# Seven-product weight groups in a fused graph network: down products in eight PSUM banks, the first group computed in full, reordered vector and scalar work

## The chip, the cores and the metric

The kernel runs on one core of a Trainium2 chip. The core has a TensorE (PE) for matrix products, a VectorE (DVE), a ScalarE (ACT), a GpSimd (POOL), and SyncE (SP), whose queue issues the loads. Each has its own instruction stream and runs it in order; they meet only at semaphores. Products land in PSUM, which has eight banks of 128 partitions x 512 floats; everything else lives in SBUF. The metric is the device time of one execution in microseconds.

## The reference, cut to what matters

```python
for i in range(L):                                   # L = 4 layers
    a = _attn(_ln(h, ln2_w[i], ln2_b[i]), cond, Wq[i], Wk[i], Wv[i], Wo[i])
    h = h + a
    u = _ln(h, ln3_w[i], ln3_b[i]) @ geglu_w[i] + geglu_b[i]     # (1024,512) @ (512,4096)
    val, gate = jnp.split(u, 2, axis=-1)
    f = val * jax.nn.gelu(gate, approximate=False)
    h = h + f @ ffo_w[i] + ffo_b[i]                              # (1024,2048) @ (2048,512)
```

Before the loop stands a graph convolution over 16384 edges, and another behind it. Nothing there is touched. All is float32. Each product of two matrices is made of three matrix products in a shorter format: every operand is split in a high part (`_hi`) and the rest (`_lo`), and high x high, low x high and high x low are summed in PSUM.

## The kernel before, in words

The change is in the second half of each layer, the gated MLP, and in the first instructions of a layer.

**Tiling of the MLP.** The 2048 features are cut in eight blocks of 256, q = 0 to 7, and each block in two halves of 128, c = 0 and 1. A block needs the up product (value and gate, K = 512, 1024 rows of x as two halves of 512 columns of the moving side), the gated product f, its split, and then the down product: eight row tiles of h, t = 0 to 7, each 2 x 3 = 6 matmuls of 128x512 into one bank, which VectorE adds to h (`add_down`, L1764). The down product of block q - 1 comes behind the up products of block q.

**Sets of seven products.** Block 0 is computed in full (`mlp_step`, four steps s = 0 to 3). Blocks 1 to 7 use seven block products in place of eight, in the manner of Strassen and Winograd: one *set* is the pair (q, c), its value and gate features seen as a 2 x 2 matrix of weight blocks A11, A12, A21, A22 against a 2 x 2 matrix of x blocks. A set needs sums of the weights (S1 to S4, `weight_sums` on VectorE, L1721 to L1726) and sums of the x blocks (`t_sums`, once a layer). `set_product` on TensorE makes 7 x 6 = 42 matmuls in four banks x, y, z, v; `p1_copy` (ACT) and `set_first`, `set_last` (DVE) add the partial products and form f. Sets alternate between banks 0 to 3 and 4 to 7 (`set_banks`).

**Weights.** A set's weights arrive by four loads in `stage`, one of two slots. ACT rounds three blocks to `wg_hi` (`blocks_high`, L1014) and the four sums (`sums_high`, L1020); POOL makes both low parts (`set_low`, L643 and L646) and raises `w_ok`. SP starts the load of piece r once `w_ok` counts the pieces up to r - 2. The order in a layer is: 2 down 0, 3 and 4 the sets (1, 0) and (1, 1), 5 a piece of the next layer's attention weights (`ahead`), 6 down 1, 7 and 8 the sets of block 2, and so on.

**Order around the change.** Each engine's order is written out by hand. VectorE in block q: `set_first(q, 0)`, `set_last(q, 0)`, `set_first(q, 1)`, `weight_sums(q + 1, 0)`, `set_last(q, 1)`, the additions of tiles 0 and 1 of down product q - 1, `weight_sums(q + 1, 1)`, the additions of tiles 2 to 7. `weight_sums(q + 1, 1)` overwrites `sums_s`, so it waits until POOL has read the sums of (q + 1, 0). The eight tiles of one down product go to four banks, so that tile t of 4 to 7 waits for the addition of tile t - 4:

```python
def down_bank(q, t):
    return 4 + t % 4 if q % 2 == 0 or q == MG - 1 else t % 4
```

**Start of the MLP.** The first steps of block 0 run beside the last attention group. The rest of steps 2 and 3 (24 matmuls with 256 columns and 24 with 512) waits for `x3_low(7)` (L1644), the low part of the last row tile of x, in which VectorE comes behind `t_sums` (L1700) and `t_low` (L1705).

**Opening of a layer.** TensorE makes two V products, a transpose, a K product and then the Q product, which waits for `x2_low` on VectorE (L1635), behind `x2_high` on ACT (L869). ACT rounds the raw input of the next group (`cond_high`, L692) ahead of both.

Of the kernel before, what the change touches and what calls it, by code (L numbers as in the profile page):

```python
# [5 lines left out]
def gnn_preln_kernel(  # L6
# [82 lines left out]
    with ExitStack() as ctx:  # L89
# [594 lines left out]
        def _(act):  # L684
# [170 lines left out]
            with act.Fori(0, L) as l:  # L855
# [1517 lines left out]
```

## Time and profile before

| | us |
|---|---|
| three runs | 2591.89, 2596.22, 2599.51 |
| median | 2596.22 |
| the profiled execution | 2592.8 |
| its span, first to last instruction | 2590.9 |
| PE busy in it | 2446.0 (94%) |
| DVE, ACT, POOL busy | 1786.3, 1136.1, 703.2 |
| mean granted TensorE clock | 0.973 of full |

The profiled execution is between the fastest and the median run. A matmul's row shows how long it was in the pipeline, while the next one starts sooner: what one costs is the distance between two starts.

### The profile page before, as it was taken

How to read it: one execution, taken by the hardware profiler on the slowest of the kernel's cores; microseconds unless marked ns; L12 is line 12 of the kernel's file. 1: busy time of each engine (PE TensorE's matmuls, PEld its weight loads, DVE VectorE, ACT ScalarE, POOL GpSimd, SP SyncE). 2: the span in 40 equal slices, each digit the busy share in tenths (PEclk: the TensorE clock that was granted, in tenths of full speed). 3: DMA queues.
4: the chain of work that ended last, by engine and by line, in shares of the span. 5: the costliest groups of instructions: out<-in, count | busy, mean ns of one | idle time of the engine just before them, and what ended most of it. 6: DMA issues, size and time to landing. Idle time of an engine off the chain costs nothing.

```text
span 2590.9 us, 37159 instructions
## 1 busy us (share of the span) xinstructions
PE 2446.0 (94%) x12191; PEld 2005.9 (77%) x12191; DVE 1786.3 (69%) x3238; ACT 1136.1 (44%) x2284; POOL 703.2 (27%) x521
## 2 busy tenths in 40 slices
PE   6889999989999999989999999989999999989999
PEld 5348888877777888867778888877778888877777
DVE  8996667766665677766665677766666667766666
ACT  8964434633333434633334434643334434633333
POOL 2000000165540000155541000165540000165541
PEclk8989999999999999999999999999999999999999
DMA  2021000022110000021111100022111000022112
GB/s 74 17 82 37 33 32 33 25 66 66 54 57 34 33 33 33 25 65 59 56 61 35 33 33 33 25 65 66 53 58 34 33 32 33 25 65 66 57 54 114
DMA packets 82646, 122.44 MB, mean 47 GB/s; under 512 B 5808, under 2 KB 63536, under 8 KB 77872
## 3 DMA queue, kind: packets, MB, share of 16 engines
q1 hardware_dynamic: 82480, 120.32, 14.0%
q8 instruction: 93, 1.52, 0.2%
q14 instruction: 73, 0.60, 0.1%
HBM read 116.10 MB, written 4.19 MB: 46 GB/s over the span
## 4 chain that ended last, share of the span: by engine, by line
PE 71%; DVE 11%; issue 10%; POOL 4%; ACT 3%; DMA 1%; DVEq 0%; POOLq 0%; ACTq 0%; SPq 0%
PE ps L1828 15%; PE ps L1829 14%; PE ps L1830 14%; PE ps L2147 6%; PE ps L2151 6%; PE ps L2149 6%; PE ps L2069 2%; DVE h L1764 2%; PE ps L2086 2%; PE ps L2088 2%; DVE oh_d L1347 1%; PE ps L2083 1%; DVE sums_s L1721 1%; POOL f_lo L627 1%; PE ps L1950 1%
## 5 line engine op out<-in xcount | busy, mean ns | idle before, releaser
L545 POOL TENSOR_SCALAR veps<-mv 128x1 f32<-128x1 f32 x65 | 17.4, 268 | 1011.3 <-DVE mv L1141 1011.3
L1828 PE MATMUL ps<-wf_hi,f_hi 128*128 128x512 f32 x512 | 216.0, 422 | 48.4 <-DVE h L1764 47.1
L627 POOL TENSOR_TENSOR f_lo<-ff,f_hi 128x512 fp32r<-128x512 f32 x128 | 173.6, 1358 | 245.5 <-ACT f_hi L1039 245.5
L1829 PE MATMUL ps<-wf_lo,f_hi 128*128 128x512 f32 x512 | 210.8, 412 | 0.0
L1764 DVE TENSOR_TENSOR h<-h,ps 128x512 f32<-128x512 f32 x256 | 165.3, 683 | 65.0 <-PE ps L1830 64.9
L1830 PE MATMUL ps<-wf_hi,f_lo 128*128 128x512 f32 x512 | 210.1, 410 | 0.0
L1828 PE MATMUL ps<-cond_hi,w_hi 128*128 128x512 f32 x512 | 203.6, 398 | 0.0
L2147 PE MATMUL ps<-xT_hi,wg_hi 128*128 128x512 f32 x448 | 178.5, 398 | 25.8 <-ACT full L1045 13.3
L1828 PE MATMUL ps<-w_hi,cond_hi 128*128 128x512 f32 x512 | 201.1, 393 | 0.3 <-issue 0.2
L1829 PE MATMUL ps<-cond_lo,w_hi 128*128 128x512 f32 x512 | 200.0, 391 | 0.0
L1830 PE MATMUL ps<-w_hi,cond_lo 128*128 128x512 f32 x512 | 200.0, 391 | 0.0
L1830 PE MATMUL ps<-cond_hi,w_lo 128*128 128x512 f32 x512 | 200.0, 391 | 0.0
L1829 PE MATMUL ps<-w_lo,cond_hi 128*128 128x512 f32 x512 | 199.8, 390 | 0.0
L861 ACT ACTIVATE v_hi<-ps 128x512 fp32r<-128x512 f32 x128 | 76.3, 596 | 248.3 <-PE ps L1830 248.3
L1504 DVE TENSOR_TENSOR v_lo<-ps,v_hi 128x512 fp32r<-128x512 f32 x128 | 88.6, 692 | 130.9 <-ACT v_hi L861 130.1
L2149 PE MATMUL ps<-xT_lo,wg_hi 128*128 128x512 f32 x448 | 177.2, 396 | 0.0
L2151 PE MATMUL ps<-xT_hi,wg_lo 128*128 128x512 f32 x448 | 177.2, 396 | 0.0
L646 POOL TENSOR_TENSOR wg_lo<-sums_s,wg_hi 128x1024 fp32r<-128x1024 f32 x56 | 134.0, 2393 | 142.6 <-ACT wg_hi L1020 142.6
L1828 PEld LDWEIGHTS ps<-wf_hi,f_hi 128*128 128x128 f32 x512 | 102.2, 200 | 88.0 <-DVE h L1764 67.0
L1039 ACT ACTIVATE f_hi<-ff 128x512 fp32r<-128x512 f32 x128 | 80.9, 632 | 200.3 <-DVE ff L1752 148.9
L921 ACT ACTIVATE p_exp<-ps,nmx 128x256 f32<-128x256 f32 x256 | 118.5, 469 | 102.0 <-DVE nmx L1550 101.4
L1051 ACT ACTIVATE gel<-gel,cols_sb 128x512 f32<-128x512 f32 x112 | 81.1, 724 | 144.0 <-DVE gel L1740 140.6
(304 smaller groups left out, 6795.9 us busy)
## 6 DMA issues: line engine op xcount, KB each, us to landing
stage<-in_pieces SPq DMA_DIRECT2D x82, 512.0 KB, 3.3
stage<-in_condT SPq DMA_DIRECT2D x33, 1024.0 KB, 4.8
stage<-in_pieces SPq DMA_DIRECT2D x224, 128.0 KB, 2.6
x<-in_x SPq DMA_DIRECT2D x2, 1024.0 KB, 6.6
at_s<-at SPq DMA_DIRECT2D x1, 2048.0 KB, 6.2
at16b<-at_s SPq DMA_DIRECT2D x1, 2048.0 KB, 9.9
out<-h SPq DMA_DIRECT2D x8, 256.0 KB, 2.0
bias_row<-in_rows SPq DMA_DIRECT2D x6, 256.0 KB, 3.4
```

What stands on the lines that cost most here:

```text
L627: pool.tensor_tensor(f_lo[q % 2][:, c, half * HALF:(half + 1) * HALF], ff[:, s % 2, :], bits(f_hi[q % 2][:, c, half * HALF:(half + 1) * HA ...
L646: pool.tensor_tensor(lo[:, 3:7, :], sums_s[:, :, :], bits(hi[:, 3:7, :]), ALU.subtract).then_inc(w_ok, 1)
L921: e = act.activation(pe_[:, b, :], ps[:, S_BANK, b * M:(b + 1) * M], ACT.Exp, bias=nmx[:, b:b + 1], accum_out=rsum[:, b:b + 1])
L1051: act.activation(gel[:, e, :], gel[:, e, :], ACT.Gelu, bias=gate_bias(q, c)).then_inc(gel_ok, 1)
L1504: dve.tensor_tensor(v_lo[:, slot, mc, :], ps[:, bank, :], bits(v_hi[:, slot, mc, :]), ALU.subtract).then_inc(v_ok, 1)
L1764: dve.tensor_tensor(h[:, t, :], h[:, t, :], ps[:, down_bank(q, t), :], ALU.add)\
L1828: pe.matmul(bank, l_hi, r_hi, start=(first and i == 0), stop=False)
L1829: pe.matmul(bank, l_hi, r_lo, start=False, stop=False)
L1830: end = pe.matmul(bank, l_lo, r_hi, start=False, stop=(last and i == n - 1))
L2147: pe.matmul(ps[:, bank, :], hi[:, a, r], moving[0][:, n, :], start=(first and n == 0), stop=False, skip_group_check=True)
L2149: pe.matmul(ps[:, bank, :], hi[:, a, r], moving[1][:, n, :], start=False, stop=False, skip_group_check=True)
L2151: last = pe.matmul(ps[:, bank, :], lo[:, a, r], moving[0][:, n, :], start=False, stop=(n == 1), skip_group_check=True)
```

## The change

Six edits:

1. **Down products in eight banks.** Tiles 0 to 3 go to the banks of the set (q + 1, 0) that was just read, tiles 4 to 7 to those of (q + 1, 1). No tile waits for an addition of its own product any more; tile 4 waits until f of the second set is done. The next set's four first products wait for the additions of tiles 4 to 7, one each. Down product 7 uses the same eight banks behind down product 6.
2. **Weight sums behind additions.** Additions of tiles 0, 1 and 2 come ahead of `weight_sums(q + 1, 1)`, and POOL's `set_low` starts only when the set's four sums are done.
3. **Value in PSUM.** `set_last` writes the value's sum back to its bank, not to `o_full` in SBUF.
4. **Set (1, 0) in full:** eight products, 48 matmuls (`full_product`), without weight sums, partial copies or additions. It needs one more weight block (A21), but no sums of x.
5. **Start of the MLP reordered** on ACT, DVE and POOL; POOL's `down_low(0)` waits for `x3_low(7)`.
6. **Opening reordered:** ACT takes `v_high`, `x2_high`, `v_high`, `k_high` ahead of the two `cond_high`; VectorE has `k_low` ahead of both `cond_low`. At a layer's end TensorE waits for the addition of tile 3 of down product 7.

```diff
 def down_bank(q, t):
-    return 4 + t % 4 if q % 2 == 0 or q == MG - 1 else t % 4
+    c = t // 4 if q < MG - 1 else 1 - t // 4
+    return set_banks(min(q + 1, MG - 1), c)[t % 4]
...
 def set_low(q, c):                                             # POOL
+    full_set = (q, c) == (1, 0)
+    if not full_set:
+        pool.wait_ge(s_ok, 4 * (short_set(l, q, c) + 1))
     pool.wait_ge(a_hi_ok, SETS * l + 2 * (q - 1) + c + 1)
     pool.tensor_tensor(lo[:, 0:3, :], ...)
     pool.wait_ge(w_hi_ok, FIRST_PIECES + PIECES * l + r + 1)
-    pool.tensor_tensor(lo[:, 3:7, :], sums_s[:, :, :], ...).then_inc(w_ok, 1)
+    if full_set:
+        pool.tensor_tensor(lo[:, A21, :], stage[:, r % 2, 0:256], ...).then_inc(w_ok, 1)
+    else:
+        pool.tensor_tensor(lo[:, 3:7, :], sums_s[:, :, :], ...).then_inc(w_ok, 1)
...
-pool.wait_ge(z3_ok, NT * l + NT)
+wait_apart(pool, x3_ok, 2 + NT * l + NT)
 down_low(0)
+set_low(1, 0)
 f_low(0, 0, 0, 0)
 f_low(0, 1, 0, 1)
-set_low(1, 0)
 f_low(0, 2, 1, 0)
 f_low(0, 3, 1, 1)
 set_low(1, 1)
...
+v_high(...); x2_high(...); v_high(...); k_high(...)           # ACT, opening
 raw_here(1)
 for part in range(2):
     cond_high(1, 1, part, stage)
-v_high(...); x2_high(...); v_high(...); k_high(...)
...
 down_high(0)                                                   # ACT, start of the MLP
 t_high(1, 0)
+blocks_high(1, 0)
+a21_high()
 t_high(3, 0)
 x3_high(7)
 f_high(0, 0, 0, 0)
+gelu(1)
 t_high(2, 0)
-gelu(1)
-blocks_high(1, 0)
 f_high(0, 1, 0, 1)
 for n in (1, 3, 2):
     t_high(n, 1)
-sums_high(1, 0)
 gelu(2)
 f_high(0, 2, 1, 0)
 gelu(3)
+blocks_high(1, 1)
+sums_high(1, 1)
+f_high(0, 3, 1, 1)
 t4_high()
-f_high(0, 3, 1, 1)
-blocks_high(1, 1)
-p1_copy(1, 0)
-sums_high(1, 1)
...
-dve.scalar_tensor_tensor(value, ps[:, z, :], value_bias(q, c), pre, ...)
+dve.scalar_tensor_tensor(ps[:, z, :], ps[:, z, :], value_bias(q, c), pre, ...)
...
-dve.tensor_tensor(ff[:, 0, :], value, gel[:, 0, :], ALU.mult)
+dve.tensor_tensor(ff[:, 0, :], ps[:, z, :], gel[:, 0, :], ALU.mult)
...
 mlp_step(0)                                                    # DVE, start of the MLP
+t_low(1, 0)
 t_sums(0, (2, 4))
-t_low(1, 0)
 x3_low(NT - 1)
-t_low(3, 0)
 mlp_step(1)
 t_sums(1, (1, 3, 2, 4))
+t_low(3, 0)
 t_low(2, 0)
-weight_sums(1, 0)
+mlp_step(2)
+weight_sums(1, 1)
 for n in (1, 3, 2):
     t_low(n, 1)
-mlp_step(2)
 add_bias(NT - 1)
 mlp_step(3)
 t4_low()
-set_first(1, 0)
-weight_sums(1, 1)
-set_last(1, 0)
+for e in range(2):
+    full_set(e)
...
-    add_down(q - 1, range(2))
+    add_down(q - 1, range(3))
     weight_sums(q + 1, 1)
-    add_down(q - 1, range(2, NT))
+    add_down(q - 1, range(3, NT))
...
+def full_product():                                            # PE
+    x, y, z, v = set_banks(1, 0)
+    pe.wait_ge(w_ok, FIRST_PIECES + PIECES * l + set_piece(1, 0) + 1)
+    block_steps(z, A11, 0, moving_x(12))
+    block_steps(v, A21, 0, moving_x(12)).then_inc(x12_mm, 1)
+    block_steps(z, A12, 0, moving_x(22), first=False)
+    block_steps(v, A22, 0, moving_x(22), first=False).then_inc(u_mm, 1)
+    block_steps(x, A11, 0, moving_x(11))
+    block_steps(y, A21, 0, moving_x(11))
+    block_steps(x, A12, 0, moving_x(21), first=False)
+    block_steps(y, A22, 0, moving_x(21), first=False).then_inc(u_mm, 1)
...
+    def bank_free(i):                                          # in set_product
+        if q > 1 and c == 0:
+            pe.wait_ge(h_ffo, 64 * l + 8 * (q - 2) + 5 + i)
...
-        if t >= 4 or q == MG - 1:
-            pe.wait_ge(h_ffo, 64 * l + 8 * q + t - 3)
+        if q == MG - 1 and t < 4:
+            pe.wait_ge(h_ffo, 64 * l + 8 * q - 3 + t)
+        elif q < MG - 1 and t == 4:
+            pe.wait_ge(ff_ok, 32 * l + 4 * q + 8)
```

VectorE at the end of block 2: the f of set (2, 1), the additions of down product 1 (`h<-h,ps`) and the sums of the weights of set (3, 1) (`sums_s`), before:

```order
L1747 SCALAR_TENSOR_TENSOR o_full<-ps,cols_sb,full 128x512
L1752 TENSOR_TENSOR ff<-o_full,gel 128x512
L1754 TENSOR_TENSOR gel<-ps,full 128x512
L1757 SCALAR_TENSOR_TENSOR ff<-ps,cols_sb,gel 128x512
L1764 TENSOR_TENSOR h<-h,ps 128x512
L1764 TENSOR_TENSOR h<-h,ps 128x512
L1721 TENSOR_TENSOR sums_s<-stage 128x256
L1722 TENSOR_TENSOR sums_s<-stage 128x256
L1724 TENSOR_TENSOR sums_s<-sums_s,stage 128x256
L1726 TENSOR_TENSOR sums_s<-stage,sums_s 128x256
L1764 TENSOR_TENSOR h<-h,ps 128x512
```

and now:

```order
L1782 SCALAR_TENSOR_TENSOR ps<-ps,cols_sb,full 128x512
L1787 TENSOR_TENSOR ff<-ps,gel 128x512
L1789 TENSOR_TENSOR gel<-ps,full 128x512
L1792 SCALAR_TENSOR_TENSOR ff<-ps,cols_sb,gel 128x512
L1808 TENSOR_TENSOR h<-h,ps 128x512
L1808 TENSOR_TENSOR h<-h,ps 128x512
L1808 TENSOR_TENSOR h<-h,ps 128x512
L1756 TENSOR_TENSOR sums_s<-stage 128x256
L1757 TENSOR_TENSOR sums_s<-stage 128x256
L1759 TENSOR_TENSOR sums_s<-sums_s,stage 128x256
L1761 TENSOR_TENSOR sums_s<-stage,sums_s 128x256
L1808 TENSOR_TENSOR h<-h,ps 128x512
```

A third addition has moved ahead of the sums, and the value no longer passes through `o_full`.

GpSimd at the start of the MLP: the low parts of the down weights (`wf_lo`), of f and of the sets (1, 0) and (1, 1) (`wg_lo`), before:

```order
L552 TENSOR_TENSOR wf_lo<-stage,wf_hi 128x1024
L627 TENSOR_TENSOR f_lo<-ff,f_hi 128x512
L627 TENSOR_TENSOR f_lo<-ff,f_hi 128x512
L643 TENSOR_TENSOR wg_lo<-stage,wg_hi 128x768
L646 TENSOR_TENSOR wg_lo<-sums_s,wg_hi 128x1024
L627 TENSOR_TENSOR f_lo<-ff,f_hi 128x512
L627 TENSOR_TENSOR f_lo<-ff,f_hi 128x512
L643 TENSOR_TENSOR wg_lo<-stage,wg_hi 128x768
L646 TENSOR_TENSOR wg_lo<-sums_s,wg_hi 128x1024
```

and now:

```order
L557 TENSOR_TENSOR wf_lo<-stage,wf_hi 128x1024
L652 TENSOR_TENSOR wg_lo<-stage,wg_hi 128x768
L656 TENSOR_TENSOR wg_lo<-stage,wg_hi 128x256
L632 TENSOR_TENSOR f_lo<-ff,f_hi 128x512
L632 TENSOR_TENSOR f_lo<-ff,f_hi 128x512
L632 TENSOR_TENSOR f_lo<-ff,f_hi 128x512
L632 TENSOR_TENSOR f_lo<-ff,f_hi 128x512
L651 REGISTER_ALU
L652 TENSOR_TENSOR wg_lo<-stage,wg_hi 128x768
L659 TENSOR_TENSOR wg_lo<-sums_s,wg_hi 128x1024
```

Set (1, 0) has moved ahead of all four f, with 256 columns of A21 in the place of 1024 columns of sums; set (1, 1) still stands behind the fourth f.

## Rows read from the trace of the kernel before

**Rows 1.** The page, part 5: group, count, busy us, mean ns, idle before.

```profile
L1039 ACT ACTIVATE f_hi<-ff 128x512 fp32r<-128x512 f32 x128 | 80.9, 632 | 200.3 <-DVE ff L1752 148.9
```

**Rows 2.** Waits of PE, whole span: who waited for whom, us in total, times, longest.

```profile
PE ps L1828 <- DVE h L1764: 47.1, 24, 2.4
PE ps L1828 <- DVE xT_lo L1644: 13.5, 4, 3.4
PE ps L2147 <- ACT full L1045: 13.3, 4, 3.8
PE ps L2147 <- POOL wg_lo L646: 12.4, 8, 2.9
...
PE ps L1828 <- DVE xT_lo L1635: 5.5, 3, 2.8
```

**Rows 3.** Timeline of PE, layer 2, block 2: start us, us, instruction, idle before.

```profile
1154.32 0.39 PE L2147 MATMUL ps<-xT_hi,wg_hi 128*128 128x512 f32 x1
...
1181.68 0.39 PE L1830 MATMUL ps<-wf_hi,f_lo 128*128 128x512 f32 x1
1184.13 0.75 PE L1828 MATMUL ps<-wf_hi,f_hi 128*128 128x512 f32 x1 [2.06 <-DVE h L1764]
1184.67 0.63 PE L1829 MATMUL ps<-wf_lo,f_hi 128*128 128x512 f32 x1
...
1188.57 0.39 PE L2147 MATMUL ps<-xT_hi,wg_hi 128*128 128x512 f32 x1
```

**Rows 4.** Windows: length, busy us (x) of PE, PEld, DVE, ACT, POOL, PEclk, DMA.

```profile
1154.32:1188.57 34.25, 32.12 (x133) 25.78 (x132) 22.38 (x30) 12.01 (x16) 18.50 (x11) 0.95 0.20 63
...
1323.98:1365.21 41.23, 41.07 (x182) 33.73 (x180) 23.54 (x35) 12.55 (x16) 17.27 (x12) 1.00 0.19 65
```

**Rows 5.** Windows, blocks 2 to 6 of layers 1 to 4, summed.

```profile
sum 679.92, PE 637.12 PEld 511.63 DVE 447.81 ACT 232.91 POOL 359.54; mean PE 159.28 PEld 127.91 DVE 111.95 ACT 58.23 POOL 89.89
```

**Rows 6.** Timeline of DVE, layer 2, end of block 2.

```profile
1173.21 2.86 DVE L1752 TENSOR_TENSOR ff<-o_full,gel 128x512 f32<-128x512 f32 x1
...
1177.63 0.75 DVE L1757 SCALAR_TENSOR_TENSOR ff<-ps,cols_sb,gel 128x512 f32<-128x512 f32 x1 [0.96 <-ACT gel L1051]
...
1179.49 1.21 DVE L1721 TENSOR_TENSOR sums_s<-stage 128x256 f32<-128x256 f32 x1
1180.63 2.05 DVE L1722 TENSOR_TENSOR sums_s<-stage 128x256 f32<-128x256 f32 x1
...
1183.39 2.47 DVE L1764 TENSOR_TENSOR h<-h,ps 128x512 f32<-128x512 f32 x4
```

**Rows 7.** Timeline of POOL, the same stretch.

```profile
1173.13 2.39 POOL L646 TENSOR_TENSOR wg_lo<-sums_s,wg_hi 128x1024 fp32r<-128x1024 f32 x1 [2.58 <-ACT wg_hi L1020]
...
1179.13 1.30 POOL L627 TENSOR_TENSOR f_lo<-ff,f_hi 128x512 fp32r<-128x512 f32 x1 [1.01 <-ACT f_hi L1039]
1180.38 2.02 POOL L643 TENSOR_TENSOR wg_lo<-stage,wg_hi 128x768 fp32r<-128x768 f32 x1
```

**Rows 8.** Two instructions of the start by line: count, ns min/median/max.

```profile
L1196 DVE TENSOR_SCALAR ps<-ps x1: 299/299/299, 15.0 to 15.0; 128x128 f32<-128x128 f32 x1
...
L1198 DVE TENSOR_SCALAR chunk<-ps x1: 291/291/291, 15.4 to 15.4; 128x128 f32<-128x128 f32 x1
```

**Rows 9.** Timeline of PE, start of the MLP of layer 2.

```profile
1100.56 0.39 PE L1828 MATMUL ps<-xT_hi,wg_hi 128*128 128x256 f32 x1 [3.39 <-DVE xT_lo L1644]
...
1108.78 0.39 PE L1830 MATMUL ps<-xT_hi,wg_lo 128*128 128x512 f32 x1
```

**Rows 10.** Timeline of DVE, the same stretch.

```profile
1094.16 3.80 DVE L1700 TENSOR_TENSOR z<-z 128x768 f32<-128x768 f32 x2
...
1104.40 2.60 DVE L1705 TENSOR_TENSOR w_lo<-z,w_hi 128x768 fp32r<-128x768 f32 x1
```

**Rows 11.** Windows, from the end of the wait for x3 to set (2, 0), four layers.

```profile
sum 205.89, PE 174.44 PEld 140.56 DVE 148.65 ACT 82.61 POOL 131.41; mean PE 43.61 PEld 35.14 DVE 37.16 ACT 20.65 POOL 32.85
```

**Rows 12.** Timeline of ACT, opening of layer 3.

```profile
1370.10 1.28 ACT L692 ACT_TABLE_LOAD   x1 [8.05 <-DMA stage<-in_condT]
```

More of the change, by code:

```diff
@@ L57, in gnn_preln_kernel @@
     A11, A12, A22, S1, S2, S3, S4 = range(7)
+    A21 = S1
     DOWN_PIECE = [2, 6, 10, 14, 18, 22, 25, 28]
@@ L404, in gnn_preln_kernel @@
         pre_5 = full[:, 1, :]
-        value = o_full[:, :, :].rearrange("p a n -> p (a n)")
         @block.sync
@@ L976, in _ @@
                 k_high(UNITS * l)
+                raw_here(1)
+                for part in range(2):
+                    cond_high(1, 1, part, stage)
                 q_copy(GROUPS * l)
@@ L1047, in set_gelu, with full_gelu @@
                 def set_gelu(q, c, e):
-                    n = SETS * l + 2 * (q - 1) + c
+                    n = short_set(l, q, c)
                     wait_apart(act, sum_ok, 5 * n + (3, 5)[e])
                     act.activation(gel[:, e, :], gel[:, e, :], ACT.Gelu, bias=gate_bias(q, c)).then_inc(gel_ok, 1)
+                def full_gelu(e):
+                    x, y, z, v = set_banks(1, 0)
+                    wait_apart(act, u_mm, 6 * l + 5 + e)
+                    act.activation(gel[:, e, :], ps[:, (v, y)[e], :], ACT.Gelu, bias=gate_bias(1, 0)).then_inc(gel_ok, 1)
                 x3_high(6)
@@ L1665, in _ @@
                 v_low(UNITS * l + 1, 1, 0, V_BANK + 1)
-                cond_low(GROUPS * l + 1, 1, 0, stage)
                 k_low(UNITS * l)
-                cond_low(GROUPS * l + 1, 1, 1, stage)
+                for part in range(2):
+                    cond_low(GROUPS * l + 1, 1, part, stage)
                 v_low(UNITS * l + 2, 2, 0, V_BANK + 2)
@@ L1751, in set_last @@
                     dve.wait_ge(sum_ok, 5 * n + 4)
-                    dve.tensor_tensor(ff[:, 0, :], value, gel[:, 0, :], ALU.mult).then_inc(ff_ok, 1)
+                    dve.tensor_tensor(ff[:, 0, :], ps[:, z, :], gel[:, 0, :], ALU.mult).then_inc(ff_ok, 1)
                     dve.wait_ge(block_mm, 7 * n + 7)
@@ L1757, in set_last, with full_set @@
                     dve.scalar_tensor_tensor(ff[:, 1, :], ps[:, x, :], value_bias(q, c), gel[:, 1, :],
+                                             ALU.add, ALU.mult).then_inc(ff_ok, 1)
+                def full_set(e):
+                    x, y, z, v = set_banks(1, 0)
+                    n = 32 * l + 4 + e
+                    dve.wait_ge(f_ok, n + 1)
+                    dve.wait_ge(gel_ok, n + 1)
+                    dve.scalar_tensor_tensor(ff[:, e, :], ps[:, (z, x)[e], :], value_bias(1, 0), gel[:, e, :],
                                              ALU.add, ALU.mult).then_inc(ff_ok, 1)
@@ L2140, in mlp_step, with block_steps @@
                     mlp_product(j, a, s, 1).then_inc(u_mm, 1)
-                def block_product(bank, a, c, moving, first=True):
+                def block_steps(bank, a, c, moving, first=True):
                     hi, lo = set_place(0, c), set_place(1, c)
@@ L2152, in block_product @@
                                          skip_group_check=True)
-                    last.then_inc(block_mm, 1)
+                    return last
+                def block_product(bank, a, c, moving, first=True):
+                    block_steps(bank, a, c, moving, first).then_inc(block_mm, 1)
                 def moving_t(n):
@@ L2305, in _ @@
                 mlp_step(0, 0, 3)
-                for q in range(1, MG):
+                full_product()
+                set_product(1, 1)
+                down_product(0)
+                for q in range(2, MG):
                     for c in range(2):
@@ L2310, in _ @@
                 down_product(MG - 1)
+                pe.wait_ge(h_ffo, 64 * l + 64 - 4)
             for t in range(NT):
```

82 lines of the change are left out of this document (51 added, 31 removed).

## The prediction

> **What bounds the kernel now.** I read the page first: TensorE is busy 94% of the span, so a microsecond is won only where TensorE waits, runs at the lower clock, or has fewer matmuls. The table of TensorE's waits [rows 2] names the places that the change touches. Four are in the MLP and one at a layer's opening: 47.1 us in 24 waits for additions of the down product (L1764), 13.5 in 4 for `x3_low` (L1644), 13.3 in 4 for ACT's copy of a first product (L1045), 12.4 in 8 for low parts of set weights (L646), 5.5 in 3 for `x2_low` (L1635). Together 91.8 us.
>
> That is not all. In the timeline of TensorE [rows 3] two matmuls that follow each other start 0.43 us apart once TensorE has waited, the distance of 512 columns at 1.2 GHz. A stretch of the same work without a wait is at granted clock 1.00, and one with the wait at 0.95 [rows 4]. The unwaited stretch is 84 matmuls of two sets and 96 of two down products in 41.23 us. About 0.3 of it is the loop's turn, so one costs 0.2273 us, the 2.4 GHz level. A block (84 + 48 matmuls) should then take 30.0 us and takes 34.25 [rows 3, 4]: 2.1 waited, the other 2.1 lost at 1.2 GHz behind it. Each wait is worth about twice its row.
>
> Why TensorE waits there is in the timelines of DVE and POOL [rows 6, 7]. The last matmul ahead of the wait starts at 1181.68, and tile 6 of the down product waits for the addition of tile 2. DVE is in `weight_sums`, whose L1722 takes 2.05 us, ending just behind POOL's L643 (1180.38 + 2.02); before it `ff<-o_full,gel` took 2.86 beside POOL's L646. Both DVE instructions read two SBUF operands and end 0.3 to 0.55 us behind the POOL instruction that was running: they wait for it.
>
> **Blocks 2 to 6: the eight banks, the moved sums, the value in PSUM.** In the new order no tile of a down product waits for an addition of the same product. Count from the start of set (q, 0) as T = 0; TensorE ends the second set at 19.1 and down tile 4 starts at 24.5. It needs the second f. Before, that f ended at 1178.38 in a block that began at 1154.32, so at T = 24.1 [rows 3, 6]; it came 2.2 late through the 2.86 us instruction. With the value read from PSUM it is done by T = 21.9: a margin of 2.6 us. If the lock stayed, 0.4 would still be left.
>
> By the Trainium skill (SBUF — State Buffer, "Who interferes with whom") a DVE instruction with at most one SBUF input does not contend with GpSimd. The stretched rows agree as far as they go: both have two.
>
> The write to PSUM by DVE is seen only in the kernel's first microseconds, 299 ns against 291 for the same form to SBUF [rows 8]. For 512 elements I take nothing; the bounds are 0 and four times the difference, 0.03 us, off the path.
>
> The next set's banks need the additions of tiles 4 to 7, one for each first product. DVE: tile 2 of the down product ends at T = 23.2, its addition at 24.0; the four sums then run 1.6 to 2.0 us, since POOL's `set_low` now waits for them, and end by 26.0. Tiles 3 to 5 are added by 28.0 at 0.62 us each (four in 2.47, [rows 6]), 6 at 29.5, 7 at 30.9. The set needs the first at 30.0 and the last at 34.1. Nothing is late. The weights of set (q + 1, 1): sums to 26.0, ACT's rounding to 27.1, POOL 2.0 and 2.4 [rows 7] to about 30.3, needed at 39.5. So a block costs 30.0, and five in four layers 600 of the 679.9 measured [rows 5]. **Saved: 80 us.**
>
> **Start of the MLP, until x3 is there.** TensorE waits 3.39 us for L1644 [rows 9]. DVE got there late: `t_sums` took 3.80 for two [rows 10], one of them held by POOL's `down_low(0)`, and `t_low` was held again. POOL now waits for `x3_low(7)`. From 1094.16 DVE needs 0.9 + 0.9 + 0.9 (768 columns each, from the additions' 0.62 for 512) and 0.7, with 0.1 between, and ends at 1097.6, 2.8 us sooner than before; about 0.6 of the wait is left. **Saved: 11 us** in four layers. What it costs: `down_low(0)` and all that stands behind it on POOL start 4 us later.
>
> **From there to set (2, 0).** The four layers take 205.9 us [rows 11]. Now: 8.45 for the rest of the steps (1100.56 to 1108.78 and one matmul, [rows 9]), then 48 matmuls of the full set, 42 of (1, 1), 48 of down 0, at 0.2273: 31.4. The full set has 6 matmuls more than before: 1.4 us a layer, in this sum. Its weights: POOL from 1097.75, down 2.4, three blocks 2.0, A21 0.7 (an estimate by columns from L643), ready at 1103.4 with the lock passed to and fro; TensorE comes at 1106.2. Covered by 2.8. The copy L1045 and its waits go.
>
> Set (1, 1) is the place that I think is late. Its low parts stand on POOL behind the fourth f_low. Behind 1098.5 DVE has six instructions with two SBUF inputs (four `t_sums`, two `t_low`) while POOL runs five without a pause (2.4, 2.0, 0.7, 1.3, 1.3). Rows 6 and 7 show one DVE instruction getting in per POOL instruction, no more (L1721 behind L627, L1722 behind L643). So step 2 is done at about 1108.4. Four sums, three `t_low`, the bias and step 3 take 3.7 and lose 1.3 to the third f_low: f at 1113.3. Rounding 0.63 [rows 1], f_low 1.3, then `t4_low` 1.2 against POOL, 1.9 and 2.4 for the set: ready at 1120.9. TensorE comes at 1097.75 + 8.45 + 10.9 = 1117.1. It waits 3.8, and I add 1.7 for the clock, as the trace shows behind most waits of that length. The bounds of the wait: 0, if DVE isn't held at all (ready at 1116), and 6.5, if it loses two rounds more. A layer: 8.45 + 31.4 + 5.5 = 45.3; four 181.3. **Saved: 24.6 us.**
>
> By the same section of the Trainium skill the shared port is an exclusive lock for a whole instruction, and whoever issues first has it. Taken strictly, a DVE instruction could find POOL's next one ahead each time, and the wait would be at its upper bound; the rows bear the milder reading.
>
> **Opening.** `cond_high` waited for a DMA with ACT's table load behind it until 1371.4 [rows 12]; only then came `v_high` and `x2_high`. Now the table load is paid beside the V product and `x2_low` ends at about 1374.0, when TensorE comes. Of 5.5 us in three openings [rows 2] 5.0 go; the bounds are 3 and 5.5. The two `cond_high` are needed a whole group later. At the layer's end the third addition ahead of `cond_low` moves the last loads back by 0.3 us; x2 hides it. The wait for the addition of tile 3 is long past. **Saved: 5 us.**
>
> **Sum.** 80 + 11 + 24.6 + 5 = 120.6 off the profiled execution's 2592.8: 2472.2. That execution was 3.4 under the median of the runs; I put half of it on top: 2474 us.
>
> **Rivals.**
>
> *A. No wait at set (1, 1).* DVE is held less than I think. Then 4 x 5.5 us more go: 2452. For it: the chain has slack that I counted as lock. Against: POOL without a pause for 7.7 us. 20%.
>
> *B. A new wait in each block.* Tile 4 for the second f, or the next set for an addition. The margin is 2.6 us, and each instruction of DVE behind the second set is in order. If 20 to 24 blocks wait 0.8 us: 2494; if the 1.2 GHz stretch stays behind each, 2530. For it: additions, sums and f stand in one queue. Against: the times above. 16%.
>
> *C. Slower than before.* The low parts of set (q, 1) come late, because `set_low` now waits for sums that stand behind three additions, and POOL's queue holds the attention piece and the next down weights behind it, whose loads wait on it too. Place: the first product of each set with c = 1. It decides from 9.2 us of lateness on, the margin above. To end slower by 0.3% (8 us; less than that either way this kernel's measurement can't tell from no change) it must cost 129 us in 28 blocks, 4.6 each, so a chain 14 us longer than I count: 2601 or more. 3%.
>
> *D. The change does nothing at the bound*, the clock and waits moving elsewhere: 2590. Against it: the 41.2 us stretch has the same work and no wait. 1%.
>
> The forecast itself, 2461 to 2490, has 60%. The range is 2448 to 2508: it takes in A and the milder half of B. Faster 96%, same 1%, slower 3%.
>
> **What would show it.** Steps of 30.0 us between first matmuls of sets (q, 0) and clock 1.00 from block 2 on; `ff<-ps,gel` at 0.7 us; no row of L1808 among TensorE's waits. A wait of 2 to 6 us for L659 once a layer, with starts 0.43 apart behind it. A wait for x3 of 0.4 to 1.0. It would be wrong if the period is over 31, or if TensorE waits for `ff` in the blocks.

## The result, and the profile after

The changed kernel takes 2465.85 us (median of 4 runs, 2465.01 to 2466.82) against 2594.05 (4 runs, 2591.76 to 2599.51) for the kernel before in the same comparison: ratio 0.9503, 95% interval 0.9486 to 0.9520. The profiled execution is the one of 2466.82 us. Its span is 2464.9 us against 2590.9, 126.0 less, at a granted clock of 0.990 against 0.973.

The table of TensorE's waits, the rows that answer to [rows 2]:

```profile
PE ps L2190 <- POOL wg_lo L659: 12.4, 4, 3.1
...
PE ps L1871 <- DVE xT_lo L1679: 1.9, 4, 0.5
...
PE ps L1871 <- DVE xT_lo L1670: 0.2, 1, 0.2
```

The additions (now L1808) and the copy of a first product have left the table. Of 91.8 us in the rows of before, 14.5 are left, and 12.4 of these are the new wait of set (1, 1).

Blocks 2 to 6, windows over the stretches of [rows 5], first that of layer 2 and then the sum of all four layers (length, busy us of PE, PEld, DVE, ACT, POOL, then PEclk, DMA share, GB/s):

```profile
1108.42:1258.02 149.60, 149.60 (x661) 123.87 (x660) 89.82 (x150) 58.58 (x78) 89.09 (x50) 1.00 0.22 69
...
sum 598.40, PE 598.40 PEld 495.54 DVE 359.32 ACT 234.54 POOL 356.41; mean PE 149.60 PEld 123.88 DVE 89.83 ACT 58.63 POOL 89.10
```

TensorE's busy time is now the window's whole length, at full clock. A block takes 29.92 us. DVE's busy time fell from 447.8 [rows 5] to 359.3 though its additions and sums are the same in number: most of the difference is time in which it had been held. Two of its groups, with the mean in ns (page, part 5, or the view by line), before,

```profile
L1752 DVE TENSOR_TENSOR ff<-o_full,gel 128x512 f32<-128x512 f32 x56 | 88.1, 1574 | 31.5 <-ACT gel L1051 29.7
L1722 DVE TENSOR_TENSOR sums_s<-stage 128x256 f32<-128x256 f32 x56 | 67.0, 1196 | 0.0
```

and after:

```profile
L1787 DVE TENSOR_TENSOR ff<-ps,gel 128x512 f32<-128x512 f32 x52 | 36.0, 692 | 1.8
L1757 DVE TENSOR_TENSOR sums_s<-stage 128x256 f32<-128x256 f32 x52 | 21.6, 416 | 0.0
```

Inside a block the prediction's times, counted from the start of set (q, 0), can be held against VectorE in block 2 of layer 2, which starts at 1108.42: the second f, the third addition, the last of the four sums, the last addition:

```profile
1129.57 0.75 DVE L1792 SCALAR_TENSOR_TENSOR ff<-ps,cols_sb,gel 128x512 f32<-128x512 f32 x1 [0.96 <-ACT gel L1074]
...
1131.74 0.69 DVE L1808 TENSOR_TENSOR h<-h,ps 128x512 f32<-128x512 f32 x1 [0.23 <-PE ps L1873]
...
1133.68 0.42 DVE L1761 TENSOR_TENSOR sums_s<-stage,sums_s 128x256 f32<-128x256 f32 x1
...
1138.54 0.69 DVE L1808 TENSOR_TENSOR h<-h,ps 128x512 f32<-128x512 f32 x1 [0.67 <-PE ps L1873]
```

The second f is done at T = 21.9 (forecast 21.9), the third addition at 24.0 (24.0), the sums at 25.7 (26.0), the last addition at 30.8 (30.9).

From the end of the wait for x3 to set (2, 0) a layer takes 8.44 us to the full set, and then (windows of the four layers, summed)

```profile
sum 145.04, PE 132.67 PEld 107.88 DVE 88.78 ACT 67.11 POOL 103.13; mean PE 33.17 PEld 26.97 DVE 22.20 ACT 16.78 POOL 25.78
```

so with four times 8.44 178.8 us against 205.9 [rows 11]. Inside is the wait of set (1, 1), here in TensorE's timeline of layer 2:

```profile
1082.82 0.39 PE L2194 MATMUL ps<-xT_hi,wg_lo 128*128 128x512 f32 x1
...
1086.29 0.50 PE L2190 MATMUL ps<-xT_hi,wg_hi 128*128 128x512 f32 x1 [3.08 <-POOL wg_lo L659]
...
1087.38 0.63 PE L2192 MATMUL ps<-xT_lo,wg_hi 128*128 128x512 f32 x1
1087.81 0.63 PE L2194 MATMUL ps<-xT_hi,wg_lo 128*128 128x512 f32 x1
...
1090.37 0.52 PE L2194 MATMUL ps<-w_hi,wg_lo 128*128 128x512 f32 x1
```

Seven starts 0.43 us apart follow it. The window from the start of the full set to the end of set (1, 1) shows what that does to the clock:

```profile
1072.16:1097.54 25.38, 22.30 (x91) 17.96 (x90) 14.19 (x24) 12.12 (x16) 16.45 (x9) 0.93 0.21 62
```

Why its weights are late is read from DVE and GpSimd, layer 2. DVE:

```profile
1064.68 6.24 DVE L1735 TENSOR_TENSOR z<-z 128x256 f32<-128x256 f32 x4
1070.84 2.90 DVE L1740 TENSOR_TENSOR w_lo<-z,w_hi 128x768 fp32r<-128x768 f32 x2
...
1078.38 0.74 DVE L1725 SCALAR_TENSOR_TENSOR ff<-ps,cols_sb,gel 128x512 f32<-128x512 f32 x1
```

GpSimd:

```profile
1063.93 2.41 POOL L557 TENSOR_TENSOR wf_lo<-stage,wf_hi 128x1024 fp32r<-128x1024 f32 x1 [4.91 <-DVE xT_lo L1679]
1066.29 2.03 POOL L652 TENSOR_TENSOR wg_lo<-stage,wg_hi 128x768 fp32r<-128x768 f32 x1
...
1079.86 1.29 POOL L632 TENSOR_TENSOR f_lo<-ff,f_hi 128x512 fp32r<-128x512 f32 x1 [3.30 <-ACT f_hi L1062]
1081.11 2.83 POOL L652 TENSOR_TENSOR wg_lo<-stage,wg_hi 128x768 fp32r<-128x768 f32 x1
1083.89 2.34 POOL L659 TENSOR_TENSOR wg_lo<-sums_s,wg_hi 128x1024 fp32r<-128x1024 f32 x1
```

Four small `t_sums` take 6.24 us while GpSimd runs five instructions without a pause; the last of them ends at 1070.92, behind GpSimd's fourth. Then GpSimd stands idle for 3.30 us ahead of the fourth `f_low`, with set (1, 1) queued behind it: so it looks as if the order of the queue makes the weights late. e4 tests it.

### The profile page after: what moved, and what is told of

The parts are those of the page before. It is cut to its first block, busy times and chain, and to the rows that moved or that the text cites. A ratio compares the mean times of both kernels' runs of the same rounds, so it can differ in the third digit from the quotient of the medians.

```text
span 2464.9 us, 37083 instructions
## 1 busy us (share of the span) xinstructions
PE 2397.8 (97%) x12215; PEld 1987.6 (81%) x12215; DVE 1658.9 (67%) x3202; ACT 1133.3 (46%) x2280; POOL 687.4 (28%) x521
## 4 chain that ended last, share of the span: by engine, by line
PE 83%; DVE 7%; issue 4%; POOL 3%; ACT 2%; DMA 0%; DVEq 0%; POOLq 0%; SPq 0%; ACTq 0%
PE ps L1871 17%; PE ps L1872 17%; PE ps L1873 17%; PE ps L2190 7%; PE ps L2192 7%; PE ps L2194 7%; PE ps L2112 2%; PE ps L2129 2%; PE ps L2131 2%; DVE oh_d L1382 1%; PE ps L2126 1%; PE ps L1993 1%; PE ps L1994 1%; POOL f_lo L632 1%; PE ps L1927 1%
## 5 line engine op out<-in xcount | busy, mean ns | idle before, releaser
L1808 DVE TENSOR_TENSOR h<-h,ps 128x512 f32<-128x512 f32 x256 | 170.2, 684 | 74.5 <-PE ps L1873 74.5
L632 POOL TENSOR_TENSOR f_lo<-ff,f_hi 128x512 fp32r<-128x512 f32 x128 | 166.4, 1310 | 177.7 <-ACT f_hi L1062 177.7
L2190 PE MATMUL ps<-xT_hi,wg_hi 128*128 128x512 f32 x480 | 187.9, 391 | 12.4 <-POOL wg_lo L659 12.4
L1871 PE MATMUL ps<-wf_hi,f_hi 128*128 128x512 f32 x512 | 199.2, 389 | 0.0
L1872 PE MATMUL ps<-wf_lo,f_hi 128*128 128x512 f32 x512 | 199.2, 389 | 0.0
L1873 PE MATMUL ps<-wf_hi,f_lo 128*128 128x512 f32 x512 | 199.2, 389 | 0.0
L2194 PE MATMUL ps<-xT_hi,wg_lo 128*128 128x512 f32 x480 | 188.1, 392 | 0.0
L2192 PE MATMUL ps<-xT_lo,wg_hi 128*128 128x512 f32 x480 | 187.8, 391 | 0.0
L652 POOL TENSOR_TENSOR wg_lo<-stage,wg_hi 128x768 fp32r<-128x768 f32 x56 | 108.3, 1934 | 110.3 <-DVE sums_s L1761 110.3
L1074 ACT ACTIVATE gel<-gel,cols_sb 128x512 f32<-128x512 f32 x104 | 75.4, 725 | 121.8 <-DVE gel L1775 118.4
L1591 DVE RECIPROCAL rinv<-rsum 128x2 f32<-128x2 f32 x128 | 21.3, 166 | 162.0 <-ACT p_exp L938 162.0
```

Source lines behind the costliest of these rows:

```text
L632: pool.tensor_tensor(f_lo[q % 2][:, c, half * HALF:(half + 1) * HALF], ff[:, s % 2, :], bits(f_hi[q % 2][:, c, half * HALF:(half + 1) * HA ...
L652: pool.tensor_tensor(lo[:, 0:3, :], stage[:, r % 2, 256:1024].rearrange("p (b n) -> p b n", n=256), bits(hi[:, 0:3, :]), ALU.subtract)
L1808: dve.tensor_tensor(h[:, t, :], h[:, t, :], ps[:, down_bank(q, t), :], ALU.add)\
L1871: pe.matmul(bank, l_hi, r_hi, start=(first and i == 0), stop=False)
L1872: pe.matmul(bank, l_hi, r_lo, start=False, stop=False)
L1873: end = pe.matmul(bank, l_lo, r_hi, start=False, stop=(last and i == n - 1))
```

## The experiments

The kernel before ran beside each group of experiments: 2589.11 us (7 runs) beside e1 to e4, 2590.57 (9 runs) beside e5 to e8, 2590.06 (7 runs) beside e9 to e12. Ratios are against it, with 95% intervals. The changed kernel itself ("after") was timed only in the first comparison, in which the kernel before took 2594.05 us; so a ratio of 0.952 beside its 0.950 is the kernel before being 3 to 5 us faster in the later comparisons, and runs are compared by their times. Where a difference is small, a run of the same comparison that lost nothing (e2 at 2466.12, e6 at 2465.34, e12 at 2466.74) serves as a second measure.

**e1: of the whole change, the eight banks alone (edits to the kernel before).** TensorE's waits for the banks are changed with it, as in the diff of the change.

```diff
 def down_bank(q, t):
-    return 4 + t % 4 if q % 2 == 0 or q == MG - 1 else t % 4
+    c = t // 4 if q < MG - 1 else 1 - t // 4
+    return set_banks(min(q + 1, MG - 1), c)[t % 4]
...
```

> The kernel before with the eight banks of the down products and nothing else of the change. Theory (the wait was an addition that stood behind the weight sums, and eight banks alone make most of it go): in a block counted from set (q, 0), the second f is done at T = 24.1 and down tile 4 starts at 24.5, no wait; the additions of tiles 2 to 4 end at about 29.7, 30.3, 30.9, so the next set waits about 1 us for tile 4 at T = 30. Period 31, against 34.25 before and 29.92 in the changed kernel; with the waits at the MLP's start left as they are, 24 blocks save 3.2 each: about 2594 - 75 = 2520 us, ratio 0.971. Rival (order and lock made the gain, banks are only room): the wait moves to the next set whole, with 1.2 GHz behind it, period 33.5 or more, 2575 us or more.

2523.62 us, ratio 0.9748 (0.9732 to 0.9764), 65 less than the kernel before beside it; the theory said 2520. A period is 31.1 us in all layers (one of the 20 is 30.0). The waits:

```profile
PE ps L2148 <- DVE h L1765: 18.6, 20, 1.0
PE ps L1829 <- DVE xT_lo L1645: 13.5, 4, 3.4
PE ps L2148 <- ACT full L1046: 13.2, 4, 3.8
PE ps L2148 <- POOL wg_lo L647: 11.4, 8, 1.8
```

The wait for additions has moved from the down product to the next set and is less than half as long. The two of the MLP's start are untouched.

**e2: after, with four banks again.** The edit of e1 undone, with its waits.

> The changed kernel with the down products in four banks again; sums behind three additions, value in PSUM, full first set and the reordered start stay. Theory (banks and order are two cures for one wait): the second f is done at T = 21.9, additions of tiles 0 to 2 end at 22.5, 23.1 and 24.1, tile 3 behind the sums at 26.6; tiles 4 to 7 are wanted at 24.5, 25.9, 27.2 and 28.6, so nothing waits: 2466 us within 5, no TensorE row for L1808. Rival (the eight banks did it): the wait of about 2 us and the 1.2 GHz stretch behind it come back in 20 to 24 blocks: 2545 us or more.

2466.12 us, 0.9523 (0.9507 to 0.9538): nothing lost.

**e3: after, with the sums ahead of the third addition, and GpSimd not waiting for them.**

```diff
-                    if not full_set:
+                    if (q, c) == (1, 1):
                         pool.wait_ge(s_ok, ...)
...
-                    add_down(q - 1, range(3))
+                    add_down(q - 1, range(2))
                     weight_sums(q + 1, 1)
-                    add_down(q - 1, range(3, NT))
+                    add_down(q - 1, range(2, NT))
```

> The changed kernel with only two additions ahead of the weight sums, and POOL no longer waiting for the sums before set_low (but for set (1, 1)). Theory: the sums are held by POOL again (three DVE operations of 2 us in place of 0.4) and end at T = 27.4, the addition of tile 4 at 29.2, wanted at 30.0: no wait, 2466 us within 5. Rival (the order of the sums is what made the wait go): a wait for L1808 of 1 to 2 us at the next set in 24 blocks, 2500 us or more.

2467.13 us, 0.9524 (0.9508 to 0.9540): nothing lost.

**e4: after, with set (1, 1) ahead of the fourth f on GpSimd.**

```diff
-                f_low(0, 3, 1, 1)
                 set_low(1, 1)
+                f_low(0, 3, 1, 1)
```

> The changed kernel with one swap on POOL: the low parts of set (1, 1) ahead of the fourth f_low of block 0. Theory (TensorE's one wait a layer of 3.1 us, and 1.7 us at 1.2 GHz behind it, come from POOL's queue, in which the set stands behind f): the set is ready at 1081.3, TensorE comes at 1083.05, wait and slow stretch both go: 4 x 4.8 = 19 us less, 2447 us, granted clock of that stretch 1.00. Rival (the set is held by VectorE's sums and the lock, so it is late anyway, or the later f_low holds block 1): 2460 us or more.

2452.42 us (2451.71 to 2453.21), 0.9471 (0.9455 to 0.9487), the fastest kernel of this study: 13.4 less than after, 13.7 less than e2 beside it. L659 has left the table of waits. GpSimd, layer 2:

```profile
1072.03 1.42 POOL L632 TENSOR_TENSOR f_lo<-ff,f_hi 128x512 fp32r<-128x512 f32 x1 [3.09 <-ACT f_hi L1062]
1073.89 1.88 POOL L652 TENSOR_TENSOR wg_lo<-stage,wg_hi 128x768 fp32r<-128x768 f32 x1 [0.44 <-DVE sums_s L1761]
1075.73 2.59 POOL L659 TENSOR_TENSOR wg_lo<-sums_s,wg_hi 128x1024 fp32r<-128x1024 f32 x1
1080.60 1.30 POOL L632 TENSOR_TENSOR f_lo<-ff,f_hi 128x512 fp32r<-128x512 f32 x1 [2.29 <-ACT f_hi L1062]
```

The weights are ready at 1078.3, where TensorE comes at 1079.9. From the end of the wait for x3 to set (2, 0) layer 2 takes 40.86 us instead of 44.70; over the four layers 15.1 go (the spans: 2449.8 against 2464.9). I had expected 19, wait and clock whole (4.8 a layer). The rest, 1.0 in layer 2, goes for the most part into two starts of set (1, 1) that are 0.50 and 0.43 us behind the one ahead (1085.82 and 1087.52), each followed by one of 0.34. The profile names no releaser, but the program and the rows of ACT and DVE do:

```profile
1085.18 0.59 ACT L1068 ACTIVATE full<-ps 128x512 f32<-128x512 f32 x1
...
1086.77 0.69 DVE L1772 TENSOR_TENSOR full<-ps,full 128x512 f32<-128x512 f32 x1
```

The fifth product waits for ACT's copy of the first, which stands behind `gelu` of the full set and ends at 1085.77; the sixth waits for VectorE's second addition, which ends at 1087.46. Each start comes 0.05 or 0.06 us behind. So with the weights on time ACT is next in the chain.

**e5: after, with TensorE kept busy through the wait of set (1, 1).**

```diff
+                    if q == 1:
+                        pe.wait_ge(ff_ok, 32 * l + 4)
+                        for _ in range(13):
+                            pe.matmul(ps[:, x, :], set_place(0, 0)[:, A11, 0:P], moving_x(11)[0][:, 0, :], start=True, ...)
                     pe.wait_ge(w_ok, ...)
```

> After, with 13 more matmuls of 512 columns whose results are thrown away (four layers, between the full set and set (1, 1); they start when the first set's f is there and take about 13 x 0.227 = 2.95 us, inside the wait of 3.08 us for the low weights). Theory: the 8 starts that are 0.43 us apart behind that wait come from TensorE having stood idle; with TensorE kept busy they go, 8 x 0.2 = 1.6 us a layer, 6.5 in all: 2459 to 2460, and no start 0.43 apart behind set (1, 1)'s first matmul. Rival: the chip slows these matmuls for something that belongs to set (1, 1) itself (its weights arriving, the banks, DVE and GpSimd at work beside it); then they stay, and the time is 2466. Second rival: the added matmuls end later than the wait: up to +1 us a layer, 2470.

2458.81 us (2457.44 to 2459.81), 0.9492 (0.9479 to 0.9505), 7.0 less than after and 6.5 less than e6 beside it, above the spread of each. TensorE's timeline:

```profile
1080.52 3.11 PE L2233 MATMUL ps<-xT_hi,wg_hi 128*128 128x512 f32 x13
1083.82 0.51 PE L2190 MATMUL ps<-xT_hi,wg_hi 128*128 128x512 f32 x1 [0.19 <-POOL wg_lo L659]
1084.16 0.40 PE L2192 MATMUL ps<-xT_lo,wg_hi 128*128 128x512 f32 x1
1084.40 0.40 PE L2194 MATMUL ps<-xT_hi,wg_lo 128*128 128x512 f32 x1
```

The weights come as late as in after: the set's first start is 3.52 us behind the full set's last, in after 3.47. But no starts are 0.43 us apart behind it, in none of the four layers, and from the full set to set (2, 0) they take 6.1 us less than in after. In the nine runs that have the wait with TensorE idle (after, e2, e3, e6, e8 to e12) the half-speed starts follow it in 34 of 36 cases, so four cases without are not luck. The 1.2 GHz stretch belongs to TensorE's standing still, not to the set; that it costs 6 to 7 us in four layers is shown here and not only reasoned from the distances.

**e6: after, with the value through SBUF again.**

```diff
+        value = o_full[:, :, :].rearrange("p a n -> p (a n)")
...
-                    dve.scalar_tensor_tensor(ps[:, z, :], ps[:, z, :], value_bias(q, c), pre, ...)
+                    dve.scalar_tensor_tensor(value, ps[:, z, :], value_bias(q, c), pre, ...)
...
-                    dve.tensor_tensor(ff[:, 0, :], ps[:, z, :], gel[:, 0, :], ALU.mult)
+                    dve.tensor_tensor(ff[:, 0, :], value, gel[:, 0, :], ALU.mult)
```

> After, with the value written to SBUF (o_full) and read from there again, as before. It has the two-operand read from SBUF back in every f. Theory of the prediction: the f of the second set comes at T = 24.1 where down tile 4 starts at 24.5, so the wait stays away or is a few tenths in some blocks: 2466 to 2470. Rival (the value in PSUM carries a good part of the gain): a wait of 0.5 to 2 us for ff with the 1.2 GHz stretch behind it in most of the 24 blocks, 2480 to 2550. Third possibility: nothing at all changes, 2466, and ff takes up to 2.9 us beside GpSimd with nobody waiting.

2465.34 us, 0.9518 (0.9505 to 0.9531): nothing lost. The theory's premise didn't come about: the second f of block 2 is done at T = 22.3, not 24.1, because its multiplication takes 1.08 us and not 2.86. Why is read in e12, which has it too.

**e7: after, with GpSimd's first down weights not waiting for x3.**

```diff
-                wait_apart(pool, x3_ok, 2 + NT * l + NT)
+                pool.wait_ge(z3_ok, NT * l + NT)
                 down_low(0)
```

> After, but GpSimd starts the low parts of the first down weights at the last z of the attention's end, not behind the last low part of x3, as before. Theory: DVE's t_sums are held again by that instruction, x3's last low part comes 2.8 us later, TensorE waits about 3.3 where it waits 0.5 now, four times: +11, 2477. What GpSimd does later starts up to 4 us earlier, so that the wait for set (1, 1) could shrink by what its own chain is not bound by DVE: by nothing if DVE sets the chain (the same TensorE wait at (1, 1), moved with x3), by up to 3.1 us and the clock's 1.6 if GpSimd sets it (then 2458 to 2466). Rival: x3's wait was never GpSimd's doing, 2466.

2473.33 us, 0.9549 (0.9535 to 0.9564), 7.5 more than after and 8.0 more than e6 beside it. The waits, with nothing left for L659:

```profile
PE ps L1871 <- DVE xT_lo L1679: 21.6, 4, 5.4
```

DVE before and at x3's last low part:

```profile
1060.08 2.80 DVE L1740 TENSOR_TENSOR w_lo<-z,w_hi 128x768 fp32r<-128x768 f32 x1
1062.81 3.96 DVE L1735 TENSOR_TENSOR z<-z 128x768 f32<-128x768 f32 x2
1066.69 1.74 DVE L1679 TENSOR_TENSOR xT_lo<-z,xT_hi 128x512 fp32r<-128x512 f32 x1
```

The wait is 5.4, not 3.3: in the new order the two parts of set (1, 0) and the first `f_low` follow the down weights on GpSimd without a pause, and DVE loses a turn to each. Behind the wait TensorE runs at half speed for a while, which it does not behind the 0.46 us of after; the distance of two starts of 256 columns is 0.21 us, where 0.12 is full speed:

```profile
1068.49 0.58 PE L1871 MATMUL ps<-xT_hi,wg_hi 128*128 128x256 f32 x1 [5.39 <-DVE xT_lo L1679]
1068.87 0.41 PE L1872 MATMUL ps<-xT_lo,wg_hi 128*128 128x256 f32 x1
1069.08 0.41 PE L1873 MATMUL ps<-xT_hi,wg_lo 128*128 128x256 f32 x1
```

From there to the full set the four layers take 7.6 us more. My +11 had the parts wrong: the wait for x3 grew by 4.9 a layer, not 2.8, the clock behind it cost another 1.9, and set (1, 1) gave back 5.0 (from the full set to set (2, 0): 31.28 for 36.26), its wait of 3.1 and the clock behind it. That makes 7.4 in four layers. Beside the old order the same edit would, to judge by the 3.4 us that the kernel before waits there, be worth less; no run shows it.

**e8: after, with the opening as before.**

```diff
+                raw_here(1)
+                for part in range(2):
+                    cond_high(1, 1, part, stage)
                 v_high(UNITS * l, 0, 0, V_BANK)
...
                 k_high(UNITS * l)
-                raw_here(1)
-                for part in range(2):
-                    cond_high(1, 1, part, stage)
...
+                cond_low(GROUPS * l + 1, 1, 0, stage)
                 k_low(UNITS * l)
-                for part in range(2):
-                    cond_low(GROUPS * l + 1, 1, part, stage)
+                cond_low(GROUPS * l + 1, 1, 1, stage)
```

> After, with the opening of a layer in the order of before (the two cond_high ahead of v_high and x2_high on ACT, one cond_low ahead of k_low on DVE). Theory: the wait for x2_low comes back in three openings, 5.5 us in all, now 0.2: 2471, +5. Rival: the wait moves elsewhere or was already covered by the other edits (the steps before it end earlier by themselves): 2466 to 2467.

2468.75 us (2465.25 to 2472.86), 0.9529 (0.9516 to 0.9542). By the times it can't be told from after. The profile has the wait back, but shorter than in [rows 2]:

```profile
PE ps L1871 <- DVE xT_lo L1670: 3.4, 3, 1.5
```

So the opening's edit is worth 3.2 us of waiting here, not 5.3. e1, which has the old opening too, waits 3.3 there: the other 2 us went with the blocks' edits, of which e1 has only the banks. In the time these 3.2 us are not clear of the spread.

**e9 to e12: the block's three edits in the combinations that are left.** Each undoes those of e2, e3 and e6 that its name doesn't keep, together.

> After with two of the three block edits undone together: two additions ahead of the sums and GpSimd's set_low not waiting for them, and the value through SBUF. Left in the blocks: the eight banks. Each of the two undone alone cost nothing. Theory (the edits cover for each other; banks alone leave a wait of about 0.9 us in most blocks, because the f beside GpSimd and the sums take turns again): a period like that of the kernel before with eight banks alone, 31.1 against 29.92, 20 periods: +24, 2490. Rival (the edits are idle each by itself and together, the eight banks carry all of it): 2466, period 29.9.

> After with all three block edits undone (four banks, sums ahead and GpSimd free, value through SBUF); the start of the MLP and the opening stay as changed. Theory: the blocks are those of before, 34.25 against 29.92 a period, 20 periods, +87: 2553. Rival (the earlier start of the MLP, not the block edits, put the blocks in a better phase): clearly less, 2466 to 2520.

> After with four banks and with the sums ahead; left in the blocks: the value in PSUM. Theory: f is 2.2 us earlier than before, so additions 0 and 1 and the sums are, too; the sums still take turns with GpSimd (3.9 us for two of them and what follows), the third addition ends at T = 27.7 where down tile 6 would start at 27.2: a wait of about 0.5 in most blocks, and some of it again for the clock: a period of 30.4 to 30.9, 2476 to 2486. Rival 1 (the value in PSUM alone is enough): 2466. Rival 2 (it does nothing, the sums beside GpSimd set the wait): 2540 to 2553.

> After with four banks and the value through SBUF; left in the blocks: the third addition ahead of the sums and GpSimd's wait for them. Theory: GpSimd's set_low, which stretched the f to 2.9 us before, now runs behind the sums, so that no f meets it (with the value in SBUF and eight banks the mean was 0.87 us against 1.57 before); nothing is late, 2466 to 2470. Rival (the f is stretched again in most blocks and with four banks TensorE waits for it): 2500 to 2553.

| kept of banks, order, value | us | ratio, 95% interval | period in layer 2, us |
|---|---|---|---|
| all three (after) | 2465.85 | 0.9503 (0.9486 to 0.9520) | 29.92 |
| order, value (e2) | 2466.12 | 0.9523 (0.9507 to 0.9538) | 29.92 |
| banks, value (e3) | 2467.13 | 0.9524 (0.9508 to 0.9540) | 29.95 |
| banks, order (e6) | 2465.34 | 0.9518 (0.9505 to 0.9531) | 29.92 |
| order (e12) | 2466.74 | 0.9524 (0.9508 to 0.9540) | 29.92 |
| value (e11) | 2485.67 | 0.9596 (0.9580 to 0.9612) | 30.50 |
| banks (e9) | 2491.10 | 0.9617 (0.9601 to 0.9633) | 31.15 |
| none (e10) | 2553.45 | 0.9865 (0.9849 to 0.9882) | 34.26 |

e9 to e11 came within 2 us of the figure that the theory gave, or inside its range, and e12 with nothing lost. The blocks' edits are worth 87.6 us (e10 less after). The order alone gives 86.7, and any two of the three give all; the value alone gives 67.8, the banks alone 62.3. (The order is two things, the third addition and GpSimd's wait for the sums; they were not taken apart.) Why the order is enough stands in DVE's groups of e12, to be held against those of before:

```profile
L1787 DVE TENSOR_TENSOR ff<-o_full,gel 128x512 f32<-128x512 f32 x52 | 45.2, 870 | 1.8
...
L1757 DVE TENSOR_TENSOR sums_s<-stage 128x256 f32<-128x256 f32 x52 | 21.6, 415 | 0.0
```

The sums run while GpSimd's `set_low` waits for them. The f still meets `set_low`, but at another point. Before, GpSimd's part of 1024 columns started 0.08 us ahead of the multiplication, which took 2.86 us (1173.13 and 1173.21, [rows 6, 7]). In e12 the multiplication comes towards the end of the shorter part, gets in between the two and takes 1.08; GpSimd's second part takes 2.85 instead of 2.4, and nobody waits for that:

```profile
1126.28 1.08 DVE L1787 TENSOR_TENSOR ff<-o_full,gel 128x512 f32<-128x512 f32 x1
...
1124.95 1.85 POOL L652 TENSOR_TENSOR wg_lo<-stage,wg_hi 128x768 fp32r<-128x768 f32 x1 [3.15 <-DVE sums_s L1761]
1126.77 2.85 POOL L659 TENSOR_TENSOR wg_lo<-sums_s,wg_hi 128x1024 fp32r<-128x1024 f32 x1
```

In e9, with the eight banks but the old order, both are long again:

```profile
L1788 DVE TENSOR_TENSOR ff<-o_full,gel 128x512 f32<-128x512 f32 x52 | 79.2, 1523 | 1.8
L1758 DVE TENSOR_TENSOR sums_s<-stage 128x256 f32<-128x256 f32 x52 | 62.3, 1198 | 0.0
```

So the banks let TensorE live with a late DVE, and the order makes DVE be on time.

e10 also gives the rest of the change: with none of the three it is 36.6 us faster than the kernel before beside it, from the full first set, the start of the MLP and the opening. Of these e7 takes one wait out and e8 the opening. The full set and the rest of the start's order were never taken apart, so how their 27 us divide is not shown.

## Why the prediction was right

By its own steps, forecast against what the trace of after shows:

| step | forecast | measured |
|---|---|---|
| blocks 2 to 6 | 80 | 81.5 (679.92 - 598.40) |
| wait for x3 | 11 | 11.6 (13.5 - 1.9) |
| from there to set (2, 0) | 24.6 | 27.1 (205.9 - 178.8) |
| opening | 5 | 5.3 (5.5 - 0.2), of which its own edit 3.2 |
| sum | 120.6 | 125.5, of 126.0 between the spans |

- *Each wait is worth about twice its row.* Held in the blocks, where it carried the largest term: the period fell by 4.3 us for a wait of 2.1. e10 has it once more: 47.1 us of waits in 24, and 87.6 us of time. But the clock's part was put too high: the 12 starts behind the wait take 4.44 us (1184.13 to 1188.57, [rows 3]) where 2.72 would do, 1.7 and not 2.1. The rest went in short stops, the largest of 0.3 us at tile 4 of the down product, which the prediction didn't see:

```profile
1178.58 0.39 PE L1830 MATMUL ps<-wf_hi,f_lo 128*128 128x512 f32 x1
1179.03 0.50 PE L1828 MATMUL ps<-wf_hi,f_hi 128*128 128x512 f32 x1
1179.37 0.39 PE L1829 MATMUL ps<-wf_lo,f_hi 128*128 128x512 f32 x1
```

  Nor is it a general factor. Behind e9's waits of 0.93 us the window has a clock of 1.00, and a period is 1.2 longer than without; and 3 of the 20 waits of before in blocks 2 to 6 have no slow stretch behind them either.
- *The value in PSUM gives the margin of 2.6 us; if the lock stayed, 0.4 would be left.* The margin was not needed, as e6 shows. But "if the lock stayed" didn't come about with the value in SBUF either, since the order shifts GpSimd's long part behind f (e12). I had booked three edits as one cure with three parts; they are three cures, and the order is the only one that suffices alone. The prediction priced the group rightly and its members not at all; that the sum came out right says nothing for the three shares.
- *The write to PSUM costs at most 0.03 us.* 759 ns in after against 750 for the same form to SBUF in e6: 0.01.
- *Set (1, 1) waits 3.8 and 1.7 for the clock.* The place, the releaser and the clock behind it held. The wait is 3.08; the 12 steps behind it take 4.44 us where 2.72 would do, so the clock costs 1.7. The weights are ready 22.5 us behind the end of the wait for x3, where I counted 23.15; this 0.7 a layer makes it the mis-sized term, 2.5 of the 4.9 us by which the sum was short. DVE lost its turns almost as counted (6.24 us for four `t_sums`).
- *The full set's weights are covered by 2.8.* They are ready at 1069.20 by the row of 1068.28 and L656's 0.92, and TensorE comes at 1072.16: 3.0.
- *The table load is paid beside the V product.* It was paid even ahead of it, at 1297.75, with the V product's end 4.4 us later.
- Rival A (no wait at set (1, 1), 2452) was not what happened, but it is what e4's two exchanged lines make of the kernel: 2452.42. Rivals B, C and D show in no row.

The result is 8.2 us under the forecast: 4.9 by the sum, 0.5 outside these steps, 1.8 by the half of 3.4, rounded up, that I had put on top because the profiled execution of before was under its median, and 1.0 because that of after is above its own (2466.82 against 2465.85).

## What to carry to other kernels

Where two engines hold each other up, look first at the order in which they meet: an order in which GpSimd's long instructions no longer start just ahead of DVE's urgent ones did here what more banks and a moved operand do together, and the single undoings (e2, e3, e6) would each have been read as "worth nothing". Undo edits to one bottleneck together as well as singly. And before an instruction queues behind another on an in-order engine, ask which of the two is needed first: exchanging two lines on GpSimd won another 13 us.

## What I had not expected of the hardware

- A half-speed stretch follows most waits of 2.0 to 3.1 us, and not all: 17 of the 20 in blocks 2 to 6 of before, 34 of the 36 of 3.1 us for set (1, 1) over nine runs. It is mostly 7 or 8 starts 0.43 us apart and costs 1.7 us; a few times it was 12 or 13 and cost 3.0. Behind the 21 waits of 0.93 us in e9 there is none. What decides in the single case is not shown. Useless matmuls in the wait remove it (e5): 6.5 to 7 us for 52 of them.
- DVE and GpSimd with two SBUF operands each take turns, one instruction each, however short the DVE one is: a sum of weights takes 415 ns alone and 1.2 us on the mean beside GpSimd. The Trainium skill (SBUF — State Buffer, "Who interferes with whom") calls the port an exclusive lock and says that whoever issues first has it. The traces agree with the lock. That DVE could be shut out altogether while GpSimd runs without a pause is not what they show.
- The starts around a stop cost about 0.1 us beyond the wait, also where the clock stays up (after the 3.08 us of set (1, 1) as after e9's 0.93 the first matmul's row is 0.50 instead of 0.39, and the next starts 0.33 behind it).
